# A two-layer gated cross-attention block: a new program by halves, with the softmax's maximum subtracted by VectorE from PSUM

## The reference

```python
x = x + jnp.tanh(g_xattn[0]) * _L0_xattn_ref(_layernorm(x), ctx, ctx, Wq, Wk, Wv, Wo, bo, mask)   # 16 heads of 64, causal
x = x + jnp.tanh(g_ffn[0]) * _L0_ffn_ref(_layernorm(x), gate_w, expert_bias, w1, w2)   # top 2 of 12 experts, 8 real of width 256, silu
x = x + jnp.tanh(g_xattn[1]) * _L1_xattn_ref(_layernorm(x), ctx, ctx, ...)             # 16 heads of 8
x = x + jnp.tanh(g_ffn[1]) * _L1_ffn_ref(_layernorm(x), ...)                           # top 2 of 8 experts of width 64 (pairs), 2 shared
# attention:  softmax(q k^T * scale + mask, axis=-1) v, then @ Wo + bo
```

## Time and profile before

| what | value |
|---|---|
| three runs | 386.68, 389.2, 391.06 us (median 389.2) |
| the profiled execution: span from first to last instruction | 386.0 us |
| granted clock of TensorE, mean | 0.977 of full speed |
| busy, of the span: PE, DVE, ACT, POOL | 82%, 68%, 46%, 42% |
| instructions | 5539 |

### The profile page before, as it was taken

How to read it: one execution, slowest core, us unless ns; L and a number is a source line. 1 busy time by engine, 2 the same in 40 slices (tenths; PEclk the granted TensorE clock), 3 DMA queues, 4 the chain that set the end, 5 groups by cost and what they waited for, 6 DMA issues and landing times. The chain is left out here.

```text
span 386.0 us, 5539 instructions
## 1 busy us (share of the span) xinstructions
PE 317.2 (82%) x1616; PEld 224.5 (58%) x1616; DVE 264.4 (68%) x624; ACT 177.2 (46%) x677; POOL 160.9 (42%) x163
## 2 busy tenths in 40 slices
PE   0798999999987978989989896867979777788964
PEld 0476777778775757765656554634655545455532
DVE  4649575665877767526546568879998969838544
ACT  2264737173636171733324356436676543542120
POOL 6226254260714452323352565746656735521100
PEclk9999999999998999999999996989999989999999
DMA  5901010101010100260025004000000000040041
GB/s 168 282 1 42 15 42 14 41 14 42 17 39 16 41 14 4 40 236 0 0 45 191 0 0 132 2 15 1 18 16 4 1 2 3 2 101 13 2 109 54
DMA packets 15443, 17.17 MB, mean 44 GB/s; under 512 B 3724, under 2 KB 12044, under 8 KB 15416
## 3 DMA queue, kind: packets, MB, share of 16 engines
q1 hardware_dynamic: 13088, 10.47, 9.3%
q10 hardware_dynamic: 2328, 6.38, 5.8%
HBM read 16.23 MB, written 0.61 MB: 44 GB/s over the span
## 5 line engine op out<-in xcount | busy, mean ns | idle before, releaser
L368 POOL TENSOR_TENSOR probs_n<-probs,rsum 128x512 f32<-128x512 f32 x64 | 68.4, 1069 | 134.5 <-DVE rsum L771 132.0
L498 ACT ACTIVATE probs<-bank,nmax 128x128 f32<-128x128 f32 x256 | 91.3, 384 | 53.1 <-DVE nmax L764 52.9
L764 DVE TENSOR_REDUCE nmax<-bank 128x4 f32<-128x512 f32 x64 | 43.8, 685 | 24.5 <-PE bank L1158 24.0
L1190 PE MATMUL bank<-id_sb,probs_n 128*128 128x128 f32 x256 | 42.0, 288 | 21.1 <-POOL probs_n L368 20.8
L498 ACT ACTIVATION_READ_ACCUMULATOR probs<-bank,nmax 128x1 f32 x256 | 57.2, 224 | 0.0
L1190 PEld LDWEIGHTS bank<-id_sb,probs_n 128*128 128x128 f32 x256 | 29.6, 144 | 41.4 <-POOL probs_n L368 35.0
L631 ACT ACTIVATE hid<-bank 128x512 f32<-128x512 f32 x42 | 24.7, 598 | 39.8 <-PE bank L1082 34.6
L1205 PE MATMUL bank<-probsT,vpad 128*128 128x128 f32 x256 | 35.5, 283 | 6.0 <-DVE oT L792 4.1
L1205 PEld LDWEIGHTS bank<-probsT,vpad 128*128 128x128 f32 x256 | 32.3, 196 | 10.3 <-DVE probsT L777 6.3
L1208 PE MATMUL bank<-probsT,kpad 128*32 128x128 f32 x256 | 35.7, 285 | 0.5 <-DVE oT L795 0.5
L1158 PE MATMUL bank<-kpad,qT 128*128 128x256 f32 x128 | 33.7, 387 | 0.0
(11 more groups left out here) (123 smaller groups left out, 619.9 us busy)
## 6 DMA issues: line engine op xcount, KB each, us to landing
gbc<-gate_dram ACTq DMA_DIRECT2D x12, 512.0 KB, 6.4
w_raw<-in_w SPq DMA_DIRECT2D x8, 384.0 KB, 3.1
gbc<-in_f0w SPq DMA_DIRECT2D x1, 1024.0 KB, 6.3
ew<-in_f0w SPq DMA_DIRECT2D x1, 1024.0 KB, 8.8
wo_st<-in_wo SPq DMA_DIRECT2D x8, 128.0 KB, 2.1
w_raw<-in_wqk SPq DMA_DIRECT2D x8, 128.0 KB, 3.0
gbc<-in_f1w SPq DMA_DIRECT2D x1, 640.0 KB, 4.6
x_sb<-in_x SPq DMA_DIRECT2D x2, 256.0 KB, 3.1
```

The source lines that it names most:

```text
L368: g.tensor_tensor(probs_n[:, t % 2], probs[:, t % 2], rsum[:, t % 2, :].unsqueeze(2).to_broadcast([P, H4, P]), ALU.mult).then_inc(a["probs ...
L498: sc.activation(probs[:, t % 2, h, :], heads(S_BANK[t % 2])[:, h, :], ACT.Exp, bias=nmax[:, t % 2, h:h + 1], accum_out=sums[:, t % 2, h:h + 1]
L764: v.tensor_reduce(nmax[:, t % 2, :], heads(S_BANK[t % 2]), X, ALU.max, negate=True).then_inc(a["nmax"], 1)
L1190: ins = nc.tensor.transpose(heads(T_BANK[t % 2])[:, hd, :], probs_n[:, t % 2, hd, :], id_sb[:])
```

## The change

The program is written anew. What it does:

- Layer 0's attention is a loop over sixteen units u (half, group, pair of sequences). The mask still enters PSUM by bf16 identity matmuls; scores then use 64 rows of the array for each head (`scores0`). VectorE takes the maximum and writes scores minus maximum from PSUM to SBUF (`tile_max`, `shift`); PE transposes that (`turn0`), and ScalarE's exponential of a whole bank of 512 is at the same time the copy out of PSUM (`exp0`). Values go to quarters of 32 output columns, and a matmul with ones gives each head's row sums (`outputs0`); VectorE divides at the end (`normalise`). The output projection is done once per half and pair, over all heads (`output0`).
- The experts of layer 0 put tokens on the output partitions, and VectorE adds gate times output into `x_sb` in four operations of 128 columns, so neither broadcast gates nor GpSimd sums are needed.
- Layer 1's attention has one step per sequence with all sixteen heads, on strips of 32 rows: 24 rows hold the three split parts, four more rows hold the maximum. Scores are computed once to find the maximum (`scores1`, `max1`), the maxima are transposed (`maxima1`) and added to the queries' extra rows (`shift1`), and scores are computed again, transposed, with the maximum already off (`turned1`). Keys and queries get into strips through DRAM (`split_heads`, `place_heads`, on SP's queue).
- Layer 1's experts stay ten steps; the first half's logits now follow the last attention sequence, and the gates' way through DRAM is on SP's queue instead of ScalarE's.

The core of the diff:

```diff
+            def split_heads(dram, hi, lo, parts, sent):
+                for c in range(3):
+                    sp.dma_start(dram[:, DH1 * c:DH1 * (c + 1), :], (hi, lo)[parts[c]].bitcast(F32)).then_inc(sent, 16)
+                sp.wait_ge(sent, 48)
+
+            def place_heads(dst, dram, tok, moved):
+                for j in range(4):
+                    sp.dma_start(dst[32 * j:32 * j + 24, :, tok].bitcast(F32),
+                                 dram.rearrange("(j i) r t -> j r i t", j=4)[j]).then_inc(moved, 16)
...
-            def normalise(a, s, t, flat=False):
-                pool.wait_ge(a["rsum"], HB * s + t + 1)
-                if t >= 2 or flat and s:
-                    pool.wait_ge(a["probsT_p"], HB * s + t - 1)
-                g.tensor_tensor(probs_n[:, t % 2], probs[:, t % 2],
-                                rsum[:, t % 2, :].unsqueeze(2).to_broadcast([P, H4, P]), ALU.mult
-                                ).then_inc(a["probs_n"], 1)
...
-            def softmax(a, s, t, flat=False):
-                act.wait_ge(a["nmax"], HB * s + t + 1)
-                if t >= 2 or flat and s:
-                    act.wait_ge(a["probs_n"], HB * s + t - 1)
-                for h in range(H4):
-                    sc.activation(probs[:, t % 2, h, :], heads(S_BANK[t % 2])[:, h, :], ACT.Exp,
-                                  bias=nmax[:, t % 2, h:h + 1], accum_out=sums[:, t % 2, h:h + 1]
-                                  ).then_inc(a["exp"], 1)
...
+            def exp0(u, b):
+                act.wait_ge(turned, 2 * u + b + 1)
+                if u:
+                    act.wait_ge(o_full, u)
+                sc.activation(PT[:, b], TP[:, b, :].rearrange("p (h q) -> p h q", h=H4), ACT.Exp).then_inc(expd, 1)
...
+            def tile_max(u, b):
+                dve.wait_ge(scores, u + 1)
+                if u:
+                    dve.wait_ge(shifted, 2 * (u - 1) + b + 1)
+                v.tensor_reduce(nmax[:, b].rearrange("p (r a) -> p r a", r=2), by_head(b), X, ALU.max, negate=True
+                                ).then_inc(maxed, 1)
+
+            def shift(u, b):
+                dve.wait_ge(maxed, 2 * u + b + 1)
+                if u:
+                    dve.wait_ge(turned, 2 * (u - 1) + b + 1)
+                v.tensor_tensor(S_sb[:, b].rearrange("p (r a) k -> p r a k", r=2), by_head(b),
+                                nmax[:, b].rearrange("p (r a) -> p r a", r=2).unsqueeze(3).to_broadcast([P, 2, 2, P]), ALU.add
+                                ).then_inc(shifted, 1)
+
+            def normalise(u):
+                g, w = u // 2 % G, u % 2
+                dve.wait_ge(o_full, u + 1)
+                if u:
+                    dve.wait_ge(o_done, u)
+                v.reciprocal(R[:], OC[:, 1, 0:2 * P]).then_inc(o_sum, 1)
+                dve.wait_ge(o_sum, u + 1)
+                if u >= 8:
+                    wait_full(dve, ("y0", 0, w))
+                v.tensor_tensor(oT[:, 2 * g:2 * g + 2, 2 * P * w:2 * P * (w + 1)],
+                                OC[:, 0, :].rearrange("p (a q) -> p a q", a=2),
+                                R[:].unsqueeze(1).to_broadcast([P, 2, 2 * P]), ALU.mult).then_inc(o_done, 1)
...
+            def max1(b, j):
+                slot, k = area("s", b, j)
+                dve.wait_ge(slot_full[slot], k + 1)
+                ins = v.tensor_reduce(NM[:].rearrange("p (j r) -> p j r", r=32)[:, 2 * j:2 * j + 2, 24:28],
+                                      SLOT[slot][:].rearrange("p j (i k) -> p j i k", i=4), X, ALU.max, negate=True)
+                ins.then_inc(maxed1, 1)
+
+            def shift1(b):
+                name = ("m", b)
+                wait_full(dve, name)
+                ins = v.tensor_tensor(q1s[:, :, batch(b)], q1s[:, :, batch(b)].bitcast(F32),
+                                      ring(name)[:, 0:P].unsqueeze(1).to_broadcast([P, 4, P]), ALU.add)
+                ins.then_inc(shifted1, 1)
+
+            def normalise1(b):
+                name = ("o", b)
+                wait_full(dve, name)
+                if b:
+                    dve.wait_ge(o_done1, b)
+                v.reciprocal(R1[:], ring(name)[:, P:2 * P]).then_inc(o_sum1, 1)
+                dve.wait_ge(o_sum1, b + 1)
+                ins = v.tensor_tensor(oT1[:, batch(b)], ring(name)[:, 0:P], R1[:], ALU.mult)
+                ins.then_inc(o_done1, 1)
+
+            def hidden1(n):
...
+            def scores0(u):
+                s, w = u // 2, u % 2
+                pe.wait_ge(mask_done, s // G + 1)
+                if u == 0:
+                    pe.wait_ge(id_done, 1)
+                pe.wait_ge(k_ready, 2 * s + 2)
+                pe.wait_ge(q_ready, 2 * s + 2)
+                if u:
+                    pe.wait_ge(shifted, 2 * u)
+                bs = slice(HB * (s // G) + 2 * w, HB * (s // G) + 2 * w + 2)
+                for r in range(2):
+                    mm(SP[:, r, :], id_bf[:], maskb[:, bs, :].unsqueeze(2).to_broadcast([P, 2, 2, P]), start=True, stop=False,
+                       skip_group_check=True)
+                for b in range(2):
+                    o = batch(2 * w + b)
+                    for p in range(2):
+                        for r in range(2):
+                            rows = slice(DH0 * r, DH0 * (r + 1))
+                            ins = mm(SP[:, r, P * (2 * b + p):P * (2 * b + p + 1)], qT[rows, s % 2, p, o],
+                                     kT[rows, s % 2, p, o], start=False, stop=True, skip_group_check=True)
+                ins.then_inc(scores, 1)
+
+            def turn0(u, b):
+                pe.wait_ge(shifted, 2 * u + b + 1)
+                if u:
+                    pe.wait_ge(expd, 2 * (u - 1) + b + 1)
+                for i in range(H4):
+                    ins = nc.tensor.transpose(TP[:, b, P * i:P * (i + 1)], S_sb[:, b, i, :], id_sb[:])
+                ins.then_inc(turned, 1)
+
+            def outputs0(u):
+                s, w = u // 2, u % 2
+                pe.wait_ge(v_ready, 2 * s + w + 1)
+                pe.wait_ge(expd, 2 * u + 2)
+                if u:
+                    pe.wait_ge(o_done, u)
+                for b in range(2):
+                    for a in range(2):
+                        for i in range(H4):
+                            hd = 2 * (i % 2) + i // 2
+                            mm(OC[32 * hd:32 * (hd + 1), 0, P * (2 * a + b):P * (2 * a + b + 1)],
+                               v0[:, s % 2, 2 * w + b, DH0 * hd + 32 * a:DH0 * hd + 32 * (a + 1)], PT[:, b, i, :],
+                               start=True, stop=True)
+                for i in range(H4):
+                    hd = 2 * (i % 2) + i // 2
+                    ins = mm(OC[32 * hd:32 * (hd + 1), 1, 0:2 * P], ones[:], PT[:, :, i, :], start=True, stop=True)
+                ins.then_inc(o_full, 1)
...
-
-                mm(heads(sb_), id_bf[:], maskb[:, HB * h + t, :].unsqueeze(1).to_broadcast([P, H4, P]),
-                   start=True, stop=False)
-                for p in range(2):
-                    ins = mm(sb_[:, 256 * p:256 * (p + 1)], qT[:, p, P * t:P * (t + 1)],
-                             kpad[:, p, t, :, :].rearrange("p h k -> p (h k)"), start=False, stop=(p == 1))
-                ins.then_inc(a["scores"], 1)
...
-                        transposed1(HB * s + t - 2)
-                elif t >= 2:
-                    pe.wait_ge(a["probsT"], HB * s + t - 1)
-                for hd in range(H4):
-                    ins = nc.tensor.transpose(heads(T_BANK[t % 2])[:, hd, :], probs_n[:, t % 2, hd, :], id_sb[:])
-                ins.then_inc(a["probsT_p"], 1)
-
-            def values(n, s, t):
...
+            def scores1(b, j):
+                slot = slot_for("s", b, j)
+                pe.wait_ge(k_moved, 64)
+                pe.wait_ge(q_moved[b // HB], 64)
+                for i in range(4):
+                    for r in range(2):
+                        rows = slice(32 * (2 * j + r), 32 * (2 * j + r + 1))
+                        ins = mm(SLOT[slot][:, r, batch(i)], q1s[rows, i, batch(b)], k1s[rows, i, batch(b)],
+                                 start=True, stop=True)
+                ins.then_inc(slot_full[slot], 1)
+
+            def turned1(b, j):
+                slot = slot_for("t", b, j)
+                pe.wait_ge(shifted1, b + 1)
+                for i in range(4):
+                    for r in range(2):
+                        rows = slice(32 * (2 * j + r), 32 * (2 * j + r + 1))
+                        ins = mm(SLOT[slot][:, r, batch(i)], k1s[rows, i, batch(b)], q1s[rows, i, batch(b)],
+                                 start=True, stop=True)
+                ins.then_inc(slot_full[slot], 1)
+
+            def maxima1(b):
+                name = ("m", b)
+                bank = take(name)
+                pe.wait_ge(maxed1, 2 * (b + 1))
+                done(name, nc.tensor.transpose(bank[:, 0:P], NM[:], id_sb[:]))
+
+            def outputs1(b):
+                name = ("o", b)
+                bank = take(name)
```

(54 more changed lines are left out.)

1849 lines of the change are left out of this document (816 added, 1033 removed).

## The result

The changed kernel takes 363.9 us (median of 4 runs, 361.52 to 366.67), the kernel before 388.4 on the same chip (386.68 to 391.06): ratio 0.939, interval 0.932 to 0.947. Forecast were 350 us, range 298 to 400. The profiled execution took 362.33 us with a span of 360.4.

The account below looks back on a forecast made before the run. The prediction took TensorE to bound layer 0 and a chain through several engines to bound layer 1's attention. Stages of 20 + 132 + 67 + 75.5 + 52 made 346.5 us of span, plus 3.2 gave 350, range 298 to 400.

Parts of the forecast that it names:

- The unknown that carried the forecast: Layer 0's units: whether matmuls on different array quarters overlap; 10.2 us of PE without, 5.6 with full overlap, 7.3 taken.
- My reason for the middle: Small matmuls: only one's second record runs beside the next's first, halving values to 1.7 us and row sums to 0.86.
- Layer 0, 132: Layer 0's attention: sixteen units of 7.8 us, plus 6.8 and 4.8, less 4.2, together 132 us against 148.6 before.
- All under PE: Layer 0's units: VectorE's and ScalarE's work hides under PE's, with the reciprocal of 256 elements taken as 0.42 us.
- Experts of layer 0, 67: Experts of layer 0: 16 steps 50 us, plus 6.8, 2.4, waits 2.8 + 2.2 and 3; before 61.7.
- GpSimd runs eight value products beside VectorE's normalisation: 3: Experts of layer 0: GpSimd's products running beside VectorE's normalisation add 3 us to the stage.
- Layer 1's attention, 75.5: Layer 1's attention: start 6.4, seven periods 53, last sequence 6.6, hooks 2.4, exposed queries' relay 7; 75.5 us against 117.7.
- The tail, 52: Experts of layer 1: two gates' relays become exposed, 52 us after the last values matmul against 40.3 before.
- Full overlap: Rival, chance 0.17: neighbours on different quarters overlap fully, units 6.1 us and sequences 4.5, kernel 299 us.
- No overlap: Rival, chance 0.16: small matmuls run one after another or draining eats the overlap; kernel 416 us.
- slow short fp32r: Rival, chance 0.08: layer 1's 128-column fp32r matmuls cost like f32 (0.21 us), 27 us more, kernel 377.
- The reciprocal: Rival, chance 0.04: VectorE's reciprocal costs 42 ns an element, 10.8 us for 256, kernel 465 us; forecast took 0.42.

Follow-up runs that it names:

- e10: Output projection's banks read ahead of units 9 and 10's maxima, layer 0's second-half logits later, against the kernel with GpSimd's products later, queries and gates earlier: 324.1 us.
- e12: Both large reciprocals replaced by copies of the same size, against the fastest kernel (324.1 us): 320.2 us.
- e4: Only GpSimd's order changed, its value products for layer 1 placed later, against the changed kernel (363.9 us): 350.3 us.
- e7: Transposes, logits, routing and gates' turn placed earlier, so the gates' relay starts sooner, against the kernel with GpSimd's products later (350.3 us): 341.5 us.
- e1: Small matmuls of the same part of the array put in a row, in both layers, against the changed kernel (363.9 us): 380.3 us.
- e8: Layer 0's four values matmuls of one column quarter put in a row, against the kernel with GpSimd's products later (350.3 us): 363.7 us.

## Why the prediction was right in sign and range, and 14 us low

**What binds.** Right: layer 1's attention, without the chain through GpSimd and VectorE, fell to 71.7 us, 43.7 less up to its last values matmul; layer 0's gained 21.6 and the start 1.1. The experts of layer 0 gave 25.6 of it back and the tail 15.2, which leaves the 25.6 us between the two spans.

**The array.** The unknown that carried the forecast fell near its good end. Values took 0.90 us (bounds 0.85 and 3.4, taken 1.7), row sums 0.54 (0.43 and 1.7, taken 0.86), scores 1.09 (0.85 and 1.7, taken 1.3). My reason for the middle, that only the second record of a matmul can run beside the next, is refuted: four records on four quarters start within 0.02 us. For rows it is the same, two records on the two halves 0.007 us apart and a pair every 0.112. The eight scores' 1.09 is eight such pairs, 0.9, and 0.2 more: the second pair comes 0.1 late, and so does the first record behind them. The Trainium skill, "TensorE: Matmul & The Clock Gate", Part 3, gives 2.38x for three column tiles. Here four quarters give 3.9x, 0.90 us where sixteen matmuls at one quarter's pace of 0.219 would take 3.5.

**The change of tiling mode.** The prediction says that no row of this case has a price for it. The trace of the kernel before had one: behind four transposes a 32-column values record starts after 0.203 us (median of 23), a 128-column one, which keeps the mode, after 0.109 (of 15). The Trainium skill ("TensorEngine Tiling (Array Packing)", Key Properties) says that such a change drains the engine; the trace agrees, at 0.09 us a change.

**Layer 0, 132 against 127.0.** The unit was mis-sized by 1.4 us, 22 in sixteen: the small matmuls 1.3 too much, handovers that do not show 0.5, less 0.45 too little for mask and projections. By the prediction's own sum with 6.4 the stage is 16 x 6.4 + 6.8 + 4.8 - 4.2 = 110. The changed kernel gave 17 of these 22 back: e10 reaches 116.6, e12 111.9. The step that failed here is "All under PE" for VectorE, for two reasons: the reciprocal was 1.75 us and not 0.42, and I looked at VectorE's load in a unit, not at who is queued behind it on the two-bank ring. At units 8 to 10 this was the residual, and PE behind it. That the stage still came within 5 us is partly luck: 22 too much and 17 too little.

**Experts of layer 0, 67 against 87.3.** The step that failed: "GpSimd runs eight value products beside VectorE's normalisation: 3". It measured 13.6 (e4; 16 by the ratios). Without it the stage takes 70.3 us in e7, against the 64 that the other terms make. I took the overlap for a small surcharge; the rows show VectorE's normalisations and most of its routing operations standing still for most of each of GpSimd's instructions, while GpSimd is as fast as alone (5.07 us for its four in e4). The prediction had no such rows, but the Trainium skill does say it ("SBUF — State Buffer", SBUF: two separate sides): the pair of ports that VectorE and GpSimd share is an exclusive lock, held for the whole instruction. The trace agrees: 5.00 against 4.98 us. Counted instruction by instruction, the normalisations lose 3.9 us (5.00 against 1.11) and four routing operations 3.6 (4.4 against 0.8): 7.5 before any loss of clock.

**Layer 1's attention, 75.5 against 71.7.** Right by two errors that cancel. Forecast was a hole of 7 for the queries; it was 12.5, as the relay takes 11 us (split done at 256.05, first use at 267.10), not 8, and less work than I thought stands in its way. The sequences were cheaper: values and row sums 0.9 each at full clock where 1.7 stood, eight fp32r scores in 0.59 where 0.86 stood. At the lower clock the same values take 1.70 (268.55), which gave part of it back.

**The tail, 52 against 55.5.** Two relays as foreseen, the first 11.5 where 10.3 was read from the earlier trace rows. The terms that the prediction lists for this stretch (1.0, 5.5, 10.3, 12.5, 5.5, 10.3, 10) add up to 55.1, not to the 52 that it took from them; with 55.1 the forecast would have been 353. e7 shows that a place earlier hides it.

**The clock.** No term of the prediction had it: 0.86 over the span, before 0.98. PE's holes at 86, 169 and 201 us are each followed by matmuls at the lower of its two levels (behind the second, six 512-column passes take 2.71 us from 172.94, and 1.47 from 191.57). The 6.1 us between e4 and e7 are its price in one stage. In layer 1 the granted clock stays at 0.66 to 0.75 in every trace but those of the kernel before (0.94) and of e1 (0.80), whatever I removed; what would lift it is open.

**Rivals.** Full overlap is what the array did; its 299 us didn't follow. It kept the forecast's 67 for the experts, its hidden VectorE and its cost of nothing for a change of mode, and its 51.5 for layer 1 left no room for a hole of 12.5 us and the lower clock. No overlap and the slow short fp32r are out. The reciprocal lay between its ends, 6.2 ns an element of 1 and 42.

## What to carry to other kernels

Small matmuls that meet on different quarters of the array are worth an interleaved loop order: 0.056 against 0.14 us each for the same sixteen. Keep matmuls of one tiling mode together, as each change costs 0.09 us. After a change that makes PE faster, read for every wait of PE what stands ahead of the releasing instruction in its engine's queue; five edits of order alone, no arithmetic, brought 40 of this kernel's 364 us. Where VectorE works from SBUF to SBUF beside GpSimd, cost the two as one queue, and a relay through DRAM as 11 us that must stand under that much work.

## What the hardware showed that I had not expected

- VectorE's normalisations (SBUF to SBUF) stand still while GpSimd's products run: four of 0.28 us became 5.0 us beside four of 1.25, and a four-element operation 1.22 us instead of 0.16. A reciprocal of four elements was not held up (0.18 both ways).
- VectorE's reciprocal costs 6.2 ns an element (0.96 us for 128, 1.75 for 256), six times a copy.
- f32 matmuls with 32 columns run on all four quarters at once: four records within 0.02 us, the next four 0.109 later. Pairs on one quarter cost nothing extra (0.90 both ways); with runs of four only two quarters run together, and sixteen take 2.4 times as long.
- Matmuls on 64 of 128 rows run two at once just as fully: pairs 0.007 us apart, one every 0.112. Four on one half followed by four on the other took 1.64 us instead of the 1.09 of alternating ones.
- A change between whole, half and quarter tiling costs 0.09 us: three in a unit, 4.5 us in layer 0's attention.
- Matmuls on different quarters start out of program order: in e8 row sums start at 60.08, values that stand before them at 60.19 to 60.40.
- The same instructions in the same stage took 76.4 and 70.3 us in two executions, with granted clocks of 0.93 and 0.99.
